# Layer 2's causal attention: float32r score pairs on row halves in bursts, mask first, two PSUM rings

## Time and profile before

| | us |
|---|---|
| median of three runs | 4177.19 |
| the profiled execution | 4191.43 |
| its span, first to last instruction | 4189.7 |
| TensorE busy | 3803.2 (91%) |
| VectorE busy | 2944.8 (70%) |
| ScalarE busy | 2515.8 (60%) |
| GpSimd busy | 1718.0 (41%) |
| mean granted TensorE clock | 0.954 of full |

### The profile page before, as it was taken

How to read it: one execution, slowest core, us unless ns; L and a number is a source line. 1 busy time by engine, 2 the same in 40 slices (tenths; PEclk the granted TensorE clock), 3 DMA queues, 4 the chain that set the end, 5 groups by cost and what they waited for, 6 DMA issues and landing times. The chain is left out here.

```text
span 4189.7 us, 96209 instructions
## 1 busy us (share of the span) xinstructions
PE 3803.2 (91%) x25352; PEld 1928.7 (46%) x25352; DVE 2944.8 (70%) x8436; ACT 2515.8 (60%) x5347; POOL 1718.0 (41%) x1956
## 2 busy tenths in 40 slices
PE   6999999999999999999369999999999999999998
PEld 2344444444444444444135555555555555555554
DVE  4888787787878878787146766666666666666664
ACT  2777776776777777677225555555555555555554
POOL 1254544544455454444433433424334334334241
PEclk7999999999999999999679999999999999999999
DMA  3333333333433333332166556456465565564561
GB/s 64 71 72 77 73 79 67 79 78 64 83 73 79 67 79 79 66 81 49 45 99 108 105 95 119 90 96 112 86 110 103 89 117 103 88 114 93 96 111 33
DMA packets 323289, 355.30 MB, mean 85 GB/s; under 512 B 28101, under 2 KB 277371, under 8 KB 322683
## 3 DMA queue, kind: packets, MB, share of 16 engines
q1 hardware_dynamic: 320641, 347.01, 43.9%
q10 hardware_dynamic: 2048, 1.05, 0.1%
HBM read 221.08 MB, written 117.44 MB: 81 GB/s over the span
## 5 line engine op out<-in xcount | busy, mean ns | idle before, releaser
L661 DVE TENSOR_REDUCE maxima<-ps_vector 128x1 f32<-128x512 f32 x2048 | 1282.6, 683 | 275.0 <-PE ps_vector L430 269.5
L1559 DVE CUSTOM_DVE_ANT_0 ps_max<-ps_max,mask 128x128 f32<-128x128 f32 (+3 forms) x2048 | 989.8, 507 | 629.6 <-PE ps_max L1258 611.3
L1416 ACT ACTIVATE probs<-ps_exp 128x512 f32<-128x512 f32 (+3 forms) x2048 | 823.8, 440 | 895.4 <-PE ps_exp L1277 809.9
L559 ACT ACTIVATE probs<-ps_scalar 128x512 f32<-128x512 f32 x2048 | 1082.8, 600 | 293.3 <-PE ps_scalar L444 292.0
L430 PE MATMUL ps_vector<-k_op,q_op 48*128 48x512 f32 x2048 | 732.1, 451 | 130.8 <-DMA k_op<-kparts 72.8
L444 PE MATMUL ps_scalar<-q_op,k_op 50*128 50x512 f32 x2048 | 733.5, 450 | 1.3 <-DMA q_op<-mrows 0.5
L1273 PE MATMUL ps_exp<-q_op,k_op 101*128 101x512 bf16 (+3 forms) x2048 | 620.2, 304 | 65.6 <-ACT probs L1416 39.1
L1258 PE MATMUL ps_max<-k_op,q_op 99*128 99x128 bf16 (+3 forms) x2048 | 625.1, 307 | 45.5 <-issue 26.8
L430 PEld LDWEIGHTS ps_vector<-k_op,q_op 48*128 48x128 f32 x2048 | 343.9, 190 | 543.9 <-DVE maxima L661 340.9
L463 PE MATMUL ps_pv<-probs,v_op 128*32 128x512 f32 x4096 | 549.8, 609 | 0.5 <-ACT oT L571 0.5
L1704 POOL TENSOR_SCALAR neg_mean<-meanvar 128x4 f32<-128x4 f32 x64 | 12.5, 195 | 1187.2 <-DVE meanvar L1598 1131.5
(11 more groups left out here) (127 smaller groups left out, 5226.1 us busy)
## 6 DMA issues: line engine op xcount, KB each, us to landing
q_op<-qk_parts SPq DMA_DIRECT2D x192, 256.0 KB, 5.4
qk_parts<-qparts SPq DMA_DIRECT2D x128, 384.0 KB, 3.3
q_op<-qk_parts SPq DMA_DIRECT2D x384, 128.0 KB, 6.1
k_op<-qk_parts SPq DMA_DIRECT2D x384, 128.0 KB, 6.6
qk_parts<-qparts SPq DMA_DIRECT2D x64, 512.0 KB, 4.2
xin<-in_x SPq DMA_DIRECT2D x32, 512.0 KB, 4.7
xres<-in_x SPq DMA_DIRECT2D x32, 512.0 KB, 4.7
x_mid<-xo SPq DMA_DIRECT2D x32, 512.0 KB, 3.4
```

The costliest lines, as they stand in the source:

```text
L559: act.activation(probs[:, quad % 2, at:at + S], ps_scalar[:, bank_of("scalar", "exp", p, 0, par), :], ACT.Exp).then_inc(ps_out["exp"], 1)
L661: dve.tensor_reduce(at, ps_vector[:, bank_of("vector", "max", k, d, par), :], AX.X, ALU.max).then_inc(ps_out["max"], 1)
L1416: act.activation(probs[:, quad % 2, at:at + nq], ps_exp[:, bank, 0:nq], ACT.Exp).then_inc(exp_done, 1)
L1559: ins = dve.tensor_tensor_reduce(row, row, mask[:, S - keys:S], 1.0, LOWEST, ALU.add, ALU.max, at)
```

## The change

Layer 2 gets the form of layer 1, in a function `layer_causal`; `layer` and its planner tables go. Layer 1 keeps its instructions (only the names of its rings change).

- Operands are two float32r parts in three groups of rows (53 rows with the position and maximum rows), heads 0 to 7 in partitions 0 to 63 and heads 8 to 15 in 64 to 127. Loads are 12 DMAs of twice the size in place of 24. GpSimd's split has two instructions in place of four.
- A pair is a maximum tile and an exponent tile of the same number of columns (512, 384, 256, 128): the maximum tiles now run from the longest to the shortest. Pairs stand in 21 bursts of two to four.
- The mask matmul comes first (`put_mask`, it starts the accumulation), and the masks of all pairs of a burst come ahead of the burst's first pair.
- Two rings: three banks for maxima, four for exponents, masks and all tasks.
- The maxima's DMAs move from ScalarE's queue to SyncE's. The feed-forward of a batch runs one body earlier, and the bias is added into x1 by GpSimd after the norm.
- `pv_tile` waits for the exponents that it reads, rather than for all of its four heads.
- The position rows come to the operands through two small DMAs to memory and six from there, once at the start.

```diff
+PLAN_CAUSAL = """
+PPP m:1:0 qk:1:1
+PPP V
+PPP V otr:2:-1
+PPP V V
+PPPP ont:0:-1 stat1:0:2 split:2:0
+PPP qk:2:1 otr:3:-1 stat1:1:2
+PP m:2:0 V
+PPP stat1:2:2 qk:3:1 stat1:3:2
+PPP ont:1:-1 V
+PPP out:0:-1 V stat2:0:-1 V
+PPP split:3:0 out:1:-1
+PPP stat2:1:-1 V
+PPP xt:0:2 V m:3:0
+PPP xt:1:2 otr:0:0 V stat2:2:-1 V
+PPP stat2:3:-1 v:0:1
+PPP otr:1:0 split:0:1 v:1:1
+PPP V qk:0:2
+PPP V m:0:1
+PPP ft:0:-1 ft:1:-1
+PPP ffn:0:-1 ffn:1:-1 V
+PPPP split:1:1 V
+"""
+BANKS_CAUSAL = (3, 4)
...
-        q_op = sb("q_op", [KB, 2 * HEADS, S], BF16)
-        k_op = sb("k_op", [KB, KHEADS, S], BF16)
+        qparts = sb("qparts", [P, 2, 2, S], F32R)
+        q_op = sb("q_op", [P, 2, HALF, S], F32R)
+        k_op = sb("k_op", [P, 2, HALF, S], F32R)
...
-        ps_exp = ctx.enter_context(nc.psum_tensor(f"ps_exp_{L}", [P, EXP_BANKS, BANK], F32))
-        ps_task = ctx.enter_context(nc.psum_tensor(f"ps_task_{L}", [P, 2, BANK], F32))
+        ps_max = ctx.enter_context(nc.psum_tensor(f"ps_max_{L}", [P, MAX_BANKS, BANK], F32))
+        ps_rest = ctx.enter_context(nc.psum_tensor(f"ps_rest_{L}", [P, REST_BANKS, BANK], F32))
...
+            def body(b, par):        # SyncE
+                load_x(b + 2, par)
+                load_maxima(b, par, 1)
+                load_residual(b - 1)
+                store_parts(b + 1, 1 - par, 1)
+                load_operands(b + 1, 1 - par, 0)
+                store_parts(b + 1, 1 - par, 2)
+                load_maxima(b, par, 2)
+                store_parts(b + 1, 1 - par, 3)
+                load_operands(b + 1, 1 - par, 1)
+                load_maxima(b, par, 3)
+                store_parts(b + 2, par, 0)
+                load_maxima(b + 1, 1 - par, 0)
+                store_out(b - 1, 1 - par)
...
+            def put_mask(p, b, par):
+                if held := held_before("rest", "exp", p, 0, b, par):
+                    pe.wait_ge(*held)
+                pe.matmul(ps_rest[:, bank_of("rest", "exp", p, 0, par), 0:P], maskb[:, :], identb[:, :],
+                          start=True, stop=False, skip_group_check=True)
+
+            def exp_tile(p, b, par):
+                pe.matmul(ps_rest[:, bank_of("rest", "exp", p, 0, par), 0:nq],
+                          k_op[at:at + KB, par, s % HALF, T * P:(T + 1) * P],
+                          q_op[at:at + KB, par, s % HALF, q0:q0 + nq],
+                          start=False, stop=True, skip_group_check=True).then_inc(ps_full["exp"], 1)
...
+            def body(b, par):        # TensorE
+                masked = 0
+                for n, (kind, k, d) in enumerate(plan):
+                    if kind == "pair":
+                        while masked < k + 1 or masked < HEADS * NT and ("pair", masked, 0) in plan[n:n + masked - k + 1]:
+                            put_mask(masked, b, par)
+                            masked += 1
+                        max_tile(k, b, par)
+                        exp_tile(k, b, par)
...
+            def max_tile(p, b, par):     # TensorE and VectorE
+                h, T = divmod(k, NT)
+                i = NT - 1 - T
...
-                pool.tensor_tensor(rest, src, parts[:, 0, :], ALU.subtract).then_inc(step, 1)
-                pool.tensor_scalar(parts[:, 1, :], rest, 1.0, 0.0, ALU.mult, ALU.add).then_inc(step, 1)
-                return pool.tensor_tensor(parts[:, 2, :], rest, parts[:, 1, :], ALU.subtract)
+                pool.tensor_scalar(parts[:, 0, :], qf[:, k % 2, :], 1.0, 0.0, ALU.mult, ALU.add).then_inc(split_step, 1)
+                pool.tensor_tensor(parts[:, 1, :], qf[:, k % 2, :], parts[:, 0, :].bitcast(F32),
+                                   ALU.subtract).then_inc(qk_split, 1)
```

More of the change, by code:

```diff
@@ L624, in body @@
                         copy_pv(k, b, par)
-                    elif kind in per and kind not in TO_VECTOR:
+                    elif kind in per and kind not in BY_VECTOR:
                         copy_task(kind, k, d, b, par)
@@ L882, in layer @@
     NQUAD = HEADS // QUAD
-    CAUSAL = L == 1
-    ALIBI = 3 if CAUSAL else 0
-    KA = QK_ROWS + ALIBI
+    L = 1
+    KA = DH * len(Q_TERMS) + ALIBI
     KB = KA + M_ROWS
     NQK = PER[L]["qk"]
[L888 to L892, removed]
+    UNIT_LOADS = 2 * len(Q_TERMS)
+    MAX_BANKS, REST_BANKS = BANKS_CAUSAL
     x_tiles = x_in.rearrange("b (t p) d -> b p t d", p=P)
     out_tiles = x_out.rearrange("b (t p) d -> b p t d", p=P)
-    per = PER[L]
-    tasks = TASKS[L]
-    flat = [(s, *t) for s in range(HEADS) for t in tasks[s]]
+    plan = read_plan(PLAN_CAUSAL)
+    per = PER[L] | {"max": HEADS * NT, "exp": HEADS * NT}
+    BY_VECTOR = ("otr", "out", "ffn")
+    RING = {"max": MAX_BANKS, "rest": REST_BANKS}
+    ring = {"max": [], "rest": []}
+    for kind, k, d in plan:
+        if kind == "pair":
+            ring["max"].append(("max", (k + 2 * QUAD * NT) % (HEADS * NT), 0 if k < 2 * QUAD * NT else 1))
+            ring["rest"].append(("exp", k, 0))
+        elif kind in per:
+            ring["rest"].append((kind, k, d))
     def valid(c):
@@ L1093, in a_head, with bank_of, held_before @@
-        def a_head(s, b, par):
-            return (b, par, s + 2 * QUAD) if s < HEADS - 2 * QUAD else (b + 1, 1 - par, s - (HEADS - 2 * QUAD))
-        def pv_quad(s, b, par):
-            return (b - 1, 1 - par, NQUAD - 1) if s < QUAD else (b, par, s // QUAD - 1)
+        def bank_of(to, kind, k, d, par):
+            return (par * len(ring[to]) + ring[to].index((kind, k, d))) % RING[to]
+        def held_before(to, kind, k, d, b, par):
+            slots, banks = ring[to], RING[to]
+            at, first = par * len(slots) + slots.index((kind, k, d)), b - par
+            bank = at % banks
+            while True:
+                if at >= banks:
+                    at -= banks
+                else:
+                    at, first = max(m for m in range(2 * len(slots)) if m % banks == bank), first - 2
+                if isinstance(first, int) and first < -2:
+                    return None
+                kind, k, d = slots[at % len(slots)]
+                c = first + at // len(slots) + d
+                if valid(c):
+                    return ps_out[kind], count(kind, c, k)
@@ L1441, in copy_task @@
                 elif kind == "ont":
[L1443 to L1445 removed]
+                    if due(seen := per["ffn"] * c):
+                        act.wait_ge(ps_full["ffn"], seen)
                     dst, src = o_cols[:, k, :], ps
```

710 lines of the change are left out of this document (213 added, 497 removed).

## The result

The changed kernel is slower: 4238.9 us as the median of four runs (4214.63 to 4246.2) against 4182.6 us before, a ratio of 1.0136 with a 95% interval of 1.0089 to 1.0182. The forecast was 4100 us and its range ended at 4225. The profiled execution, at 4214.63 us, is the fastest of the four, so the profile shows less of the loss than the runs do: its span is 23 us longer than before's, the medians differ by 56. Layer 1, whose instructions are the same, hides another part: layer 2's first setup DMA is issued at 2059.0 us where before's is at 2079.4, and in the ten other profiles it lies anywhere from 2055.9 to 2075.2. From that DMA to the end layer 2 takes 2153.8 us against 2110.2, 44 us more.

A forecast was written before the change was run, and what follows sets the result against it. TensorE's instruction stream in layer 2 was taken as the bound. Per batch 3.3 + 1.2 (ScalarE waits) + 0.9 - 3.1 = 2.3 us, 77 us with the tail: 4191 to 4114, median 4100 us; own range 4050 to 4150, with rivals 4030 to 4225.

The forecast's parts named there:

- The stream: TensorE's score work in layer 2: 21.9 us a batch against 25.2 before, 3.3 us less.
- The ring waits: New TensorE waits on ScalarE and VectorE around layer 2's bursts: 3.1 us a batch, bounds 0.5 and 8.
- The 1.0 us added for what the hand count misses: Allowance on top of 2.1 us a batch of burst waits followed in layer 2.
- The wait for the maxima goes: TensorE's layer 2 wait for the maxima's DMA goes, as they are issued ahead of operand loads: 0.9 us a batch.
- The loop's turn stays: The gap at the turn of layer 2's hardware loop stays at 1.05 us a batch.
- shortens the tail: The earlier feed-forward shortens the end of the kernel a little, taking the gain from 74 to 77 us.
- The clock: Layer 2's clock falling from 0.98 to below 0.94 was a sign of error, making every cost dearer.
- The lead-in: Layer 2's setup: six extra DMAs may cost 5 us once, halved splits return as much; put at nothing, 5 us either way.
- The slower rival, 4235 us: At layer 2's 21 burst starts, masks wait for ScalarE's previous exponents and drain the ring: 4235 us, chance 0.18.
- Short tiles: 128-column float32r pairs in layer 2 take four passes, 0.22 us each: 56 us back, 4160 us, chance 0.18.

The follow-up runs named there:

- e4: Kernel before the change with layer 2's hardware loop written out: 4060.94 us, ratio 0.9728 to the kernel before.
- e6: Changed kernel with the maxima of quads 2 and 3 sent ahead of a store and operand loads, and layer 2's loop written out: 4022.35 us, ratio 0.9665.
- e2: Changed kernel with the maxima of quads 2 and 3 sent ahead of the store of part 2 and the second half's operand loads: 4138.8 us, ratio 0.9904.
- e1: Changed kernel with the load of x moved behind quad 1's maxima and the output's store into the middle of the next body: 4265.59 us, ratio 1.0211.
- e5: Changed kernel, loop kept, with quads 2 and 3's maxima sent earlier, x's load behind quad 1's maxima, output's store behind the second operand loads: 4123.83 us, ratio 0.9910.
- e7: Changed kernel without the mask matmuls, the exponent's input scaled by 0.01, so its softmax differs: 4198.19 us, ratio 1.0099.

## Why the prediction was wrong

The time was wrong in sign, and the sum explains where. Per body, in the loop kernels, with e4 and e6 as the smooth bodies (the clock's term is an estimate: the time between 2400 and 3900 us that TensorE ran at the lower level, times the half that it lost; low clock in a gap costs nothing and is left out):

| us a body | before | after |
|---|---|---|
| smooth body (e4, e6) | 59.3 | 57.0 |
| gap at the turn | 1.05 | 2.4 |
| wait for the maxima | 0.9 | 1.8 |
| lower clock | 1.0 | 2.5 |
| waits for ScalarE beyond e4's | 0.8 | |
| sum | 63.1 | 63.7 |
| measured in the profile | 63.6 | 64.5 |

- *The stream: right.* Without their waits the smooth bodies differ by 3.4 us (59.3 less 0.45, 57.0 less 1.6), and the sum had 3.3. A burst's costs are those predicted: masks 0.06 us apart, the pair of matmuls within 0.01 us, the first pair at 0.33.
- *The ring waits: too high.* They are 1.6 us a body, not 3.1. VectorE's are 1.3 of it, 0.66 each in the two `PPPP` bursts, predicted 0.6 each. The 1.0 us added for what the hand count misses was not there. This error of 1.5 us hid a part of the others.
- *"The wait for the maxima goes" (0.9 us): the step that failed.* Two things in it were wrong. The 0.9 us of before were put down to the 24 operand loads, but they belong to quad 1 behind the turn, and vanish in e4 with the loads unchanged. And the new order was misread: "issued ahead of the loads" is not what SyncE's listing says, where the maxima of quad 2 stand behind the first six loads and a store and those of quad 3 behind the last six. I took the small transfer's time for that of a small transfer; behind 1.5 MB it takes 9 to 10 us. Quad 1's wait did go, but 1.8 us a body on quads 2 and 3 came, 1.8 us off the sum, and without them e2 is 100 us faster, the clock's share included.
- *"The loop's turn stays": failed.* It grew by 1.3 us a body, 2.7 a turn. Half is the branch, 3.7 to 5.1 us, because the earlier feed-forward puts the output's store, and with it the load of x, right ahead of the turn (e1 and e5 bring it back to 3.7). The other half is the new plan's end: the matmuls of `qk` that ran beside the branch are no longer there. I had written the earlier feed-forward down as one that shortens the tail, which it did: 28 us from the last PV to the end in place of 33.
- *The clock: not in the sum at all.* I named 0.94 as a sign of error but priced it at nothing; it fell to 0.95 and costs some 1.5 us a body more than before. In the changed kernel it fell within the gap at each of eleven turns and stayed at the lower level for some 10 us; before it fell behind seven of eleven, mostly for 3 us. With the maxima first and no turn it is 1.00 (e6), so the holes come first and the clock follows them.
- *The lead-in: put at nothing.* From layer 2's first setup DMA to its first PV pass 111 us where 97 did, 15 us once. The setup itself, to the first maximum tile, is 2 us of that; the rest lies between the first maximum tile and the first PV, and its cause stays open.
- *The slower rival, 4235 us*, came nearest the time, by luck. It had the right end, holes and then a lower clock, but the wrong place: masks waited 6.8 us of 1500 for their banks, and e7 shows that the masks were not what held it. *Short tiles* were no matter: the 128-column pair costs 0.07 us ahead of a PV and 0.11 to 0.12 ahead of another pair, where this rival needed 0.22.

With these sizes the sum's gain of 2.3 us a body becomes a loss of 0.7, against 0.9 measured: 2.3 + 1.5 for the rings - 1.8 for the maxima - 1.3 for the turn - 1.5 for the clock is -0.8, and the stream gives 0.1 back.

Open: some 9 us of e2's gain in layer 2, the longer lead-in, and what sets the 3.7 us that the branch takes with quiet queues.

## What to carry to other kernels

Here a small transfer's delay was set by the bytes queued ahead of it, not by its own size: send the small one that an engine waits for before the bulk loads, and count 10 us behind 1.5 MB. Read the order off the listing, transfer by transfer, before you write that one stands ahead of another. A hardware loop's turn waits for transfers too; keep the queues empty around it, end the body with long matmuls that run beside the branch, or make turns rare (without them the kernel before gained 117 us). When TensorE's work shrinks, ask first what will then be late: in this kernel waits at the turn and for the maxima, and the clock behind them, took 3.7 us a body more and ate the 2.3 us that the new form gives, and only with them repaired did it show (4022 us against 4061, ratios 0.9665 and 0.9728).

## What the runs showed of the hardware

- In the timeline of the changed kernel a gap of 5 us on TensorE (2772 to 2777 us) is followed by matmuls at the 1.2 GHz level, a granted clock of 0.50 from 2777 to 2783 us. Before, the gap of 2.3 us at 2776.34 us was followed by 1.00. In e6's layer 2, where the longest wait between 2400 and 3900 us is 1.0 us, the clock stayed at 2.4 GHz.
- The branch that turns a hardware loop takes TensorE's sequencer 3.7 us at the median in quiet queues (e1, e5) and 5.1 us behind 1 MB of data; the first instruction packets start 1.0 to 1.4 us after its beginning in the one case and 2.1 to 2.6 us in the other; the other four engines take 0.04 to 0.06 us for theirs. TensorE loses only what its queued matmuls don't cover: 2.25 us before, behind 1.96 us of matmuls, and 3.55 us in e5, behind a short PV.
- float32r keeps one column a cycle in short tiles too: a pair of 128 columns holds TensorE 0.07 us before the switch to PV, and one of 256 columns 0.12 us. But the 512-column pair behind a 128-column one takes 0.29 us in place of 0.23.
- A pair of 8 KB DMAs issued 3 us behind six of 256 KB in the same queue landed 9 to 10 us after its issue. With a 512 KB store moved ahead of such a pair, and the load of x later in the body, its waits rose from 8.8 to 49.9 us in 1500 (e1).
